# A decoder layer on one core: partial output products of two batches moved into the head of cross-attention, in the place of idle products

## The reference

```python
x = x + self_attention(layernorm(x))        # 8 batches x 128 tokens x 512; 128 heads of width 4, rope part of 64
x = x + cross_attention(layernorm(x), ctx)  # 32 query heads of width 16, 8 key/value heads, rotary positions
x = x + ffn(layernorm(x))                   # base matrix + top-2 of 8 low-rank experts, gated
```

## Time and profile before

| | |
|---|---|
| median of 3 runs | 816.56 us (815.79 to 816.97) |
| the profiled execution, its own time | 816.52 us |
| its span, first to last instruction | 814.8 us |
| busy share PE, DVE, ACT, POOL | 96%, 77%, 71%, 73% |
| granted TensorE clock, mean | 1.000 |

### The profile page before, as it was taken

The page is one execution under the profiler, slowest core; times in us unless marked ns, Lnnn a source line. Parts: engine busy times, 40 slices in busy tenths (PEclk is TensorE's granted clock), DMA queues, the critical chain, the costliest instruction groups (busy, mean ns, idle before and its releaser), DMA issues.

```text
span 814.8 us, 17893 instructions
## 1 busy us (share of the span) xinstructions
PE 785.9 (96%) x5641; PEld 388.4 (48%) x5641; DVE 628.3 (77%) x1190; ACT 580.2 (71%) x1070; POOL 592.5 (73%) x537
## 2 busy tenths in 40 slices
PE   4999999999999999999999999999999899999997
PEld 3465444444444444444444444444443445555543
DVE  7767676767767888867778877769887889888876
ACT  7757777777777777777777777778775567556651
POOL 7967999999988888888878888878754755222101
PEclk9999999999999999999999999999999999999999
DMA  9264345533434433344432344443322100000001
GB/s 340 101 206 139 96 138 166 144 121 82 111 97 116 107 82 80 98 96 107 121 92 79 86 97 106 122 146 75 89 54 69 35 3 2 2 15 15 15 27 40
DMA packets 52176, 75.80 MB, mean 93 GB/s; under 512 B 10256, under 2 KB 34096, under 8 KB 51616
## 3 DMA queue, kind: packets, MB, share of 16 engines
q1 hardware_dynamic: 52128, 75.23, 33.1%
HBM read 38.69 MB, written 19.40 MB: 71 GB/s over the span
## 4 chain that ended last, share of the span: by engine, by line
PE 84%; DVE 7%; DMA 3%; SPq 2%; issue 2%; ACT 2%; POOL 0%; DVEq 0%
PE PS L1570 39%; PE PS L1644 7%; PE PS L1611 7%; PE PS L1645 7%; PE PS L1507 6%; PE PS L1659 5%; PE PS L1745 2%; DVE xm L1311 1%; PE PS L1684 1%; PE PS L1621 1%; PE PS L1693 1%; PE PS L1843 1%; DMA KQ<-xmT 1%; PE PS L1809 1%; PE PS L1860 1%
## 5 line engine op out<-in xcount | busy, mean ns | idle before, releaser
L1570 PE MATMUL PS<-XTh,W 128*128 128x512 f16 x1024 | 346.0, 379 | 0.0
L654 POOL TENSOR_TENSOR Pl<-PR,Ph 128x512 f16<-128x512 f32 x254 | 285.8, 1156 | 28.3 <-ACT Ph L936 28.1
L929 ACT ACTIVATE PR<-PS 128x512 f32<-128x512 f32 x256 | 152.8, 597 | 131.4 <-PE PS L1645 124.7
L1125 DVE TENSOR_REDUCE mneg<-PS 128x4 f16<-128x512 f32 x256 | 171.6, 685 | 35.2 <-PE PS L1611 33.5
L1570 PE MATMUL PS<-XTl,W 128*128 128x512 f16 x512 | 193.6, 378 | 0.0
L1113 DVE SCALAR_TENSOR_TENSOR QS<-PS,QC 64x512 f16<-64x512 f32 x256 | 175.5, 685 | 20.3 <-ACT QC L846 16.3
L846 ACT ACTIVATE QC<-PS 64x512 f16<-64x512 f32 x256 | 150.7, 589 | 6.5 <-PE PS L1570 1.6
L1570 PEld LDWEIGHTS PS<-XTh,W 128*128 128x128 f16 x1024 | 96.5, 97 | 119.1 <-issue 25.9
L936 ACT ACTIVATE Ph<-PR 128x512 f16<-128x512 f32 x256 | 139.3, 617 | 0.0
L1611 PEld LDWEIGHTS PS<-KC,QC 112*128 112x128 f16 x1024 | 78.4, 97 | 63.5 <-DVE mneg L1125 2.8
L1611 PE MATMUL PS<-KC,QC 112*128 112x128 f16 x1024 | 99.4, 219 | 0.8 <-ACT QC L846 0.7
(11 more groups left out here) (236 smaller groups left out, 1027.4 us busy)
## 6 DMA issues: line engine op xcount, KB each, us to landing
Wraw<-in_wqr SPq DMA_DIRECT2D x32, 512.0 KB, 4.5
QS<-QC SPq DMA_DIRECT2D x64, 256.0 KB, 3.1
head_outputs<-OS SPq DMA_DIRECT2D x256, 40.0 KB
q_content_parts<-stg SPq DMA_DIRECT2D x12, 256.0 KB, 2.9
k_content_parts<-stg SPq DMA_DIRECT2D x12, 256.0 KB, 3.4
QC<-q_content_parts SPq DMA_DIRECT2D x116, 24.0 KB
KC<-k_content_parts SPq DMA_DIRECT2D x29, 96.0 KB
xs<-in_x SPq DMA_DIRECT2D x8, 256.0 KB, 4.7
```

The lines of the kernel that those rows point to most:

```text
L654: nc.gpsimd.tensor_tensor(Pl[:, 4 * j.s + b], PR[:, b], Ph[:, 4 * j.s + b], ALU.subtract).then_inc(s_pl, 1)
L929: nc.scalar.activation(PR[:, b, :], PS[:, bB[b % 2], :], ACT.Exp, scale=ATT_SCALE).then_inc(s_e, 1)
L1125: nc.vector.tensor_reduce(mneg[:, j.p, j.s, :, b], PS[:, bA[b % 2], :].rearrange("p (j k) -> p j k", j=GH), AX.X, ALU.max, negate=True).th ...
L1570: last = mm(PS[:, bQ[c], :], wt[:, j.w, k, c * P:(c + 1) * P], xt[:, k, sl], start=(i == 0), stop=(i == 3 * KT - 1))
```

## The change

The orders of PE, DVE and POOL between self-attention and u = 5, and at u = 27 and 28, are rewritten. The parts of batches 6 and 7 go to u = -5 to 4 of the loop, in bank 7; `keep_clock` is gone; the outputs of batches 0 and 1 go between the scores of job 63; batches 2 and 3 use banks 4 and 5; DVE's steps for batches 0 to 3 are spread over u = -8 to -1; POOL takes the power of batch 0 before its last subtraction and splits two weight matrices later; one of the last base products is pulled forward from u = 28 to 27.

```diff
-        LOWS_AT = {-5: [(0, 0), (0, 1)], -3: [(0, 2), (0, 3)], 3: [(2, 0)], ...
+        LOWS_AT = {-3: [(0, 0), (0, 1)], -1: [(0, 2), (0, 3)], 3: [(2, 0)], ...
-        SUMS_AT = {0: 4, 5: 5, 8: 6, 13: 7}
+        SUMS_AT = {0: 4, 5: 5, 8: 6, 12: 7}
         def o1_bank(v):
-            return v if v < B // 2 else bF[1]
+            return (0, 1, 4, 5)[v] if v < B // 2 else bF[1]
+        def part_bank(v):
+            return v - B // 2 if v < B - 2 else bF[1]
 # GpSimd
-            for n in range(NH - 3, NH):
+            for n in range(NH - 3, NH - 1):
                 p_low(job(n))
+            p_low(job(NH - 1), 0, 3)
+            inverse(1, 0)
+            p_low(job(NH - 1), 3, 4)
 # VectorE
             o_out(job(NH - 3))
-            x1_part(6)
-            x1_part(7)
-            o_out(job(NH - 2))
             normalise(KT - 1, 0)
-            normalise(KT - 1, 1)
             x1(0)
 ...
+                if u == -1:
+                    x1_part(6)
+                if u == 4:
+                    x1_part(7)
 ...
                 if u == FIRST:
+                    normalise(KT - 1, 1)
+                if u == FIRST + 1:
+                    o_out(job(NH - 2))
                     rope_factors()
-                if u == FIRST + 1:
+                if u == FIRST + 2:
+                    k_rope(0)
+                    o_out(job(NH - 1))
+                if u == FIRST + 3:
                     x1(1)
-                    k_rope(0)
-                if u == FIRST + 2:
-                    o_out(job(NH - 1))
                     normalise(KT - 1, 2)
+                if u == FIRST + 4:
                     normalise(KT - 1, 3)
-                if u == FIRST + 3:
                     x1(2)
-                if u == FIRST + 4:
+                if u == -1:
                     x1(3)
 # TensorE, ahead of the loop
             scores(job(NH - 2), 2)
             pe.wait_ge(s_m, 4 * NH)
-            output_part(6, 0)
             scores(job(NH - 2), 3)
-            output_part(6, 1)
             weigh(job(NH - 3))
-            output_part(6, 2)
-            scores(job(NH - 1), 0)
-            output_part(7, 0)
-            scores(job(NH - 1), 1)
-            output_part(7, 1)
-            scores(job(NH - 1), 2)
-            output_part(7, 2)
-            scores(job(NH - 1), 3)
+            for i in range(4):
+                scores(job(NH - 1), i)
+                if i < KT - 1:
+                    output(0, i)
+            output(1, 0)
+            output(1, 1)
+            output(0, KT - 1)
+            output(1, 2)
             weigh(job(NH - 2))
-            for v in range(2):
-                for T in range(KT):
-                    output(v, T)
+            for T in range(KT - 1):
+                output(2, T)
 # TensorE, in the loop over u
-            SCORES_FIRST = (1, 4, 5, NU - 5)
+            SCORES_FIRST = (5,)
                 if u == -2:
-                    pe.wait_ge(s_x1, B // 2 - 1)
+                    pe.wait_ge(s_x1, 1)
                     pe.wait_ge(s_kx, 2)
+                if u == 0:
+                    pe.wait_ge(s_x1, B // 2)
 ...
                 if r == 1 and 0 <= b - 3 < B:
-                    take(bF[1], s_x3, b - 2)
-                    base(b - 3, 0)
+                    if u == NU - 4:
+                        base(b - 3, 1)
+                    else:
+                        take(bF[1], s_x3, b - 2)
+                        base(b - 3, 0)
 ...
+                if u == 4:
+                    output_part(7, 2)
+                if u == NU - 5:
+                    take(bF[1], s_x3, B - 3)
+                    base(B - 4, 0)
 ...
                     if u == -2:
-                        pe.wait_ge(s_oe, NH)
-                        keep_clock(2)
-                    if u == 2:
-                        keep_clock(3)
+                        output_part(6, 1)
+                        x_rough(0)
+                        output(3, KT - 1)
                     norm_turn(1, b + 2, bF[0])
                 if u == FIRST + 2:
+                    output(1, KT - 1)
                     weigh(job(NH - 1))
+                if u == FIRST + 3:
                     for T in range(KT - 1):
-                        output(2, T)
-                if u == FIRST + 3:
+                        output(3, T)
+                    pe.wait_ge(s_oe, NH)
+                    output_part(6, 0)
                     output(2, KT - 1)
-                    for T in range(KT):
-                        output(3, T)
-                if -1 <= u <= 2:
-                    keep_clock(3)
-                if u == -2:
-                    pe.wait_ge(s_x1, B // 2)
+                if u == -1:
+                    output_part(6, 2)
+                if u == 0:
+                    pe.wait_ge(s_x0, 3)
+                    output_part(7, 0)
+                if u == 1:
+                    output_part(7, 1)
-                if 0 <= u + 2 < NU:
+                if 0 < u + 2 < NU:
                     x_rough(u + 2)
```

More of the change, by code:

```diff
@@ L349, in build @@
         bF = (6, 7)
-        LOWS_AT = {-5: [(0, 0), (0, 1)], -3: [(0, 2), (0, 3)], 3: [(2, 0)], 4: [(1, 0)], 6: [(1, 1)], 7: [(1, 2)], 9: [(1, 3)]}
+        LOWS_AT = {-3: [(0, 0), (0, 1)], -1: [(0, 2), (0, 3)], 3: [(2, 0)], 4: [(1, 0)], 6: [(1, 1)], 7: [(1, 2)], 9: [(1, 3)]}
         LATER = {5: 4, 8: 5, 11: 6, 15: 7}
-        SUMS_AT = {0: 4, 5: 5, 8: 6, 13: 7}
+        SUMS_AT = {0: 4, 5: 5, 8: 6, 12: 7}
         FIRST, LAST = -2 * KT, (B + 3) * KT - 3
@@ L649, in late_values, with p_low @@
                 ).then_inc(s_vg, 1)
-            def p_low(j):
-                for b in range(3 if isinstance(j.n, int) and j.n in BY_DVE else 4):
+            def p_low(j, b0=0, b1=4):
+                for b in range(b0, 3 if isinstance(j.n, int) and j.n in BY_DVE else b1):
                     pool.wait_ge(s_ph, 4 * j.n + b + 1)
@@ L777, in _ @@
             nc.gpsimd.memset(kst[:, :, :, :, X3], MS).then_inc(s_kx, 1)
-            for n in range(NH - 3, NH):
-                p_low(job(n))
-            pool.wait_ge(s_kx, 2)
             def inverse(n, b):
@@ L785, in inverse @@
                     nc.gpsimd.tensor_tensor(rstd[:, n, b:b + 1], rstd[:, n, b:b + 1], power[:], ALU.pow).then_inc(n_sd[n], 1)
+            for n in range(NH - 3, NH - 1):
+                p_low(job(n))
+            p_low(job(NH - 1), 0, 3)
+            inverse(1, 0)
+            p_low(job(NH - 1), 3, 4)
+            pool.wait_ge(s_kx, 2)
             done = [0]
@@ L815, in _ @@
                     nc.gpsimd.tensor_tensor(part[2], q, part[0], ALU.subtract).then_inc(s_xqr, 1)
-                if r == 2:
+                if r == 2 and b + 2 > 0:
                     inverse(1, b + 2)
@@ L1355, in x1_part @@
                 dve.wait_ge(s_o0, v - B // 2 + 1)
-                nc.vector.tensor_tensor(xs[:, v, :], xs[:, v, :], PS[:, v - B // 2, :], ALU.add).then_inc(s_x0, 1)
+                nc.vector.tensor_tensor(xs[:, v, :], xs[:, v, :], PS[:, part_bank(v), :], ALU.add).then_inc(s_x0, 1)
             def x1(v):
@@ L1428, in _ @@
                         dve.wait_ge(s_xq, v + 1)
+                        if v == 0:
+                            dve.wait_ge(s_kvr, 1)
                         if v >= 1:
@@ L1683, in output_part @@
                 pe.wait_ge(s_un, B * T + v + 1)
-                last = mm(PS[:, v - B // 2, :], U[:, T, v * S:(v + 1) * S], wo_sb[:, T, :], start=(T == 0), stop=(T == KT - 2))
+                last = mm(PS[:, part_bank(v), :], U[:, T, v * S:(v + 1) * S], wo_sb[:, T, :], start=(T == 0), stop=(T == KT - 2))
                 if T == KT - 2:
@@ L1690, in output @@
                 pe.wait_ge(s_un, B * T + v + 1)
-                if T == 0:
+                if T == 0 and v < 2:
                     pe.wait_ge(s_x0, v + 1)
+                if T == 0 and v == 2:
+                    pe.wait_ge(s_e, 4 * NH)
                 last = mm(PS[:, o1_bank(v), :], U[:, T, v * S:(v + 1) * S], wo_sb[:, T, :], start=(T == 0 or v >= B // 2),
@@ L1861, in norm_turn @@
                     last.then_inc(n_tp[n], 1)
-            def keep_clock(n):
-                for _ in range(n):
-                    mm(PS[:, bF[1], :], Wxh[:, 0, 0:P], Wxh[:, 0, :], start=True, stop=True)
             def outputs_turn(v, bank):
@@ L1886, in query @@
                         last.then_inc(s_xq, 1)
-            SCORES_FIRST = (1, 4, 5, NU - 5)
+            SCORES_FIRST = (5,)
             def late_output(v):
-                if v == B // 2:
-                    pe.wait_ge(s_oe, NH)
+                pe.wait_ge(s_x0, 4)
                 take(bF[1], s_x1, v + 1)
@@ L1930, in _ @@
                     if 0 <= b - 3 < B:
-                        base(b - 3, 1)
+                        if u != NU - 4:
+                            base(b - 3, 1)
                         base(b - 3, 2)
```

## The result

Slower: 818.93 us in the median of 18 executions (816.87 to 822.24), against 816.49 us of the kernel before (18 executions). The ratio is 1.0032, 95% interval 1.0022 to 1.0043. I had forecast 816.0, in a range from 814.2 to 818.0, and gave a slower result 0.15.

The account below looks back on a forecast made before the run. PE, busy 96% of the span, was taken as the bound. The terms 0.0 + 1.0 - 0.4 + 0.2 - 0.3 made 0.5 us faster than the profiled 816.5: 816.0, called no change, in a range from 814.2 to 818.0.

Parts of the forecast that it names:

- Head to `query(1)`: PE's starts of output(0, 3), query(0), turn(0) and query(1): 4.8, 5.6, 5.0 and 3.3 us early.
- `turn(2)`: PE at u = 0 waits 2.9 to 3.4 us for x1(3) behind rope(1); turn(2) 0.0 us early.
- u = 0 to 2: From turn(2) to x_rough(4), two fp32 products replace 12 idle ones: 1.0 us faster, bounds 0 to 2.2.
- u = 4 and 5: output_part(7, 2) fills the wait at x_scores(4), x1_part(7) adds 0.6 us on DVE: -0.4 (0 to -0.6).
- The clock: Rival: the clock falls to 1.2 GHz behind the wait ahead of turn(2), costing 2 to 4 us: 819; chance 0.08.
- 3.7 us the most that the idle products can give: Removing 17 idle fp16 products of 0.22 us each from PE gives at most 3.7 us, slightly more for waits.
- The moved `normalise`: Moving a normalise from u = 13 to 12 fills a DVE wait: 0.2 us faster.
- u = 27 and 28: Base product ahead of x_scores(27) waits for bank 7, delaying DVE and a transpose: -0.3 us (+0.6 to -0.4).
- third rival: All of batch 0 late: gather, normalisation or ACT's splits come 2.1 us later, giving 818.3 us; chance 0.07.

Follow-up runs that it names:

- the first wait filled: The changed kernel with 13 idle products on PE inside the wait ahead of `turn(2)`: 818.50 us, ratio 1.0018.
- Both: The changed kernel with x1(3) ahead of rope(1), output_part(7, 2) at u = 2 and x1_part(7) at u = 3: 813.70 us, ratio 0.9958.
- x1(3) alone moved: The changed kernel with VectorE's x1(3) ahead of rope(1) at u = -1 instead of behind it: 817.54 us, ratio 1.0007.
- u = 27 and 28 undone: The changed kernel with both new waits mended and base(4, 0) back at u = 28, x_scores(27) first: 814.03 us, ratio 0.9969.
- the moved normalise: The version with both waits mended and u = 27 and 28 as before, plus normalise(3, 4) moved from u = 0 to 2: 814.17 us, ratio 0.9975.

## Why the prediction was wrong

- *Head to `query(1)`: right.* I wrote 619.2, 626.8, 634.9 and 640.6; the trace has 619.4, 627.25, 635.25 and 640.41. ACT is busy until 633.1 and holds the query's split, as written. But I misread what it does there: of the 5.8 us in the earlier trace rows the three weight splits are 4.3, and the rest is a table load (ACT_TABLE_LOAD, 1.28) and the short ACTIVATE on `power`, which I had taken for the last split.
- *`turn(2)`: right*, 646.45 forecast, 646.08 measured, the wait 2.91 us in a forecast of 2.9 to 3.4. POOL slowed VectorE less than I allowed (0.82 us for the rope's last step instead of 1.14).
- *u = 0 to 2:* forecast 1.0 us faster. With the first wait filled and the clock at 1.00 it is 0.6 faster (8.0 us from `turn(2)` to `x_rough(4)`, before 8.6); in the profiled execution, at half clock, 0.8 slower.
- *"u = 4 and 5 ... I take -0.4 (0 to -0.6)": the first step that failed.* I counted `x1_part(7)` as 0.6 us more on VectorE and asked only who waits for VectorE's outputs behind it. But the text with the diff says that `late_output` waits for all four parts' additions, and `x1_part(7)` stands on VectorE behind `rope(2)` and `x_max(13)`. It is an addition behind a rope as at u = 0, which I had found there and missed here: a wait of 2.09 us. Here the rope waits for no query (`query(2)` ends at 660 us); VectorE is simply busy without a break from 663.1 us until the addition is done at 667.6. Between `x_rough(4)` and `late_output(4)` PE loses 2.3 us against the kernel before, before any clock is counted. Without the wait, in executions at 1.000, the kernel takes 815.9 us; with it 817.1, a difference of 1.2 us. That 815.9 lies next to my 816.0 is in part luck: `turn(2)` gave 0.4 where I had 0.0, u = 0 to 2 gave 0.6 and not 1.0, the moved `normalise` and u = 27 and 28 were both too small.
- *The clock: the second step that failed.* My sum has nothing for it. I gave its fall 0.08, because "at both ends of the rest PE works without a break"; by the mean clocks it fell in 13 of 18 executions. The executions at full clock, 817.1, lie inside my range, the median of all, 818.9, outside. One fall I priced at 2 to 4 us, from "a stretch of 3 to 5 us of products" that no row showed; the trace has about 3 and about 7 us at half clock. By the traces the first fall costs 1.4 us. The second costs 1.9: from `late_output(4)` to `project_outputs(0)` it is 5.69 us, 3.78 in the trace with that wait gone. The groups of executions lie further apart, by 1.8 and 2.6 us. That the groups are one fall and two is likely, since there are two places; only an execution of the last group has a trace, and the rest of the difference is open.
- *The Trainium skill* (TensorE: Matmul & The Clock Gate, section HAM oscillation) has an array that waits between bursts of products start the next burst at half clock. The traces agree in that: 0.50 behind the waits of 2.91 and 2.09 us. The rests in its example are longer than these, so the measured ones decide here. I had given the rival a small chance for want of a row.
- *"3.7 us the most that the idle products can give":* true as a bound, but it looks at one side only. Taking them out of the kernel before, with nothing in their place, costs 1.1 us. I had read them as work to be saved, and only their absence showed what they bought.
- *The moved `normalise`:* forecast 0.2 us faster. PE gains 0.4 at u = 15 in the traces of the changed kernel and of the versions with one or both waits mended; no run has that move alone.
- *u = 27 and 28:* the waits came as described (0.6 and 0.75 us), 0.5 us lost in the trace against my 0.3; in the times nothing is resolved.
- *A slip in the third rival:* 816.0 and 2.1 make 818.1, not 818.3. Nothing hangs on it.

Open: what decides in one execution whether the clock falls. "Both" has PE busy 2.42 of 4 us at 646 to 650 us, and its clock held in five of five executions. With x1(3) alone moved it is 2.32 of 4, and it fell behind that in the profiled one. But with u = 27 and 28 undone the stretch is the same as in "both", 2.42 of 4, and there two of six executions, on another chip, have the lower mean clock. I have not separated chance, the chip and the product at 651 us that follows.

## What to carry to other kernels

When a step is moved behind another on an engine that works in order, look for every wait on its semaphore, not only for the one that the change is about; here one pattern (an addition that stands behind a rope) stood at two places. Work put into a wait for its own sake can be an investment in the clock: before taking idle products out, find the rests that they covered, and give the place real work of the same density or leave some of them. Look at the mean clock of each execution, not only at the median time: here the three groups of times go with it.

## What the runs showed of the hardware

Hardly expected: the granted clock falls to 0.50 at a wait of 2 to 3 us, and also behind waits of 0.9 to 1.7 us that lie close together (x1(3) first; idle products out; the moved normalise). In the profiled execution of the changed kernel it stays there for about 3 and about 7 us (646.4 to 649.8, 666.8 to 673.7), most of it dense work. Executions of one program differ: a mean clock of 0.998 or less in 13 of 18 with the two waits, in 11 of 11 with the idle products gone, in 2 of 68 of the kernel before unchanged. A fall costs 1.4 us where it lasted from 646 to 650 us, and 1.9 us at the second wait.
